# Causal attention in a 16-head, four-layer kernel: first-pass scores dealt to the steps of the second pass by a table

## The chip, the cores and the metric

The program runs on one core of a Trainium2 chip. A core has TensorE (PE in the profile), VectorE (DVE), ScalarE (ACT), GpSimd (POOL) and SyncE (SP), which here only issues DMAs. The metric is the device time of one execution in microseconds.

## The reference

Four layers are chained, each followed by a layer norm over 2 x 2048 tokens of 256 channels: causal attention with 16 heads of 16, an FP4-quantised linear layer, a second causal attention, and two blocks of local attention with a gated feed-forward. The change touches the two causal attentions, which share one function:

```python
q = (x @ Wq).reshape(b, t, h, d) * scale      # t = 2048, h = 16, d = 16
k = (x @ Wk).reshape(b, t, h, d) * scale
v = (x @ Wv).reshape(b, t, h, d)
dot = jnp.einsum('bqhd,bkhd->bhqk', q, k)
dot = jnp.where(causal[None, None], dot, -jnp.inf)
attn = jax.nn.softmax(dot, axis=-1)
out = jnp.einsum('bhqk,bkhd->bqhd', attn, v).reshape(b, t, h * d)
return out @ Wo
```

## The kernel before

The program loops twice over the batch and runs both causal attentions in each turn, so `attend` runs four times. Each time `project` has left q and k as three bf16 parts in `parts`, and six products of parts are stacked into 96 rows for the score matmuls (`stack_q`, `stack_k`). The 16 heads are four groups of four. A group's stacks are 48 DMAs (`load_stack`, L815); there are two sets of stacks, used in turn, and the first group's are loaded in `project`.

**Items and steps.** An item (`ITEMS`) is one group with one chunk of 512 queries: 16 items, with chunks 0, 1, 2, 3 in groups 0 and 2 and 3, 2, 1, 0 in groups 1 and 3. So the items have 4, 8, 12, 16, 16, 12, 8, 4, 4, 8, 12, 16, 16, 12, 8, 4 steps (`STEPS`, 160, numbered from 0). A step is one tile of 128 keys. The last four steps of an item lie on the diagonal, and there the width falls from 512 to 384, 256 and 128 queries. The text calls the last three of these the narrow steps of an item, and the other steps full.

**Second pass, the steps.** For each step PE makes scores with keys on the partitions, for four heads (L690, in two pairs of heads). ACT takes the exponential of each pair (L722) into one of two `probs` buffers. In the next step PE multiplies them with the values (L667, `pv`). For a diagonal block, POOL zeroes the masked half in between (L615). At an item's end ACT copies the outputs out of their bank (L714).

**First pass, the slots.** The exponential needs the row maximum to be taken off, and this rides as three extra rows of `stack_q`. So before an item's steps its maxima must be known. `first_pass_slots` lists the work: a slot fills one of three PSUM banks with scores that have queries on the partitions (L648, with a mask by L651), and DVE reads the bank once and keeps its maximum (L761 or L756). An item with chunk c has 11 + 16c such slots. After them comes a slot "maxima" (PE L638; DVE L776 to L785), in which DVE turns the maxima into three bf16 rows. After an item's end comes a slot "outputs" (PE L632, DVE L794 and L796). There are 560 score slots, 16 for maxima and 16 for outputs. PE may run three banks ahead of DVE (L627), and both take the slots in one order.

**What sets the place of a slot.** The list is fixed; the plan says how many slots go in front of step 0 and how many into each step. Before, the plan is computed (L92 to L107): each slot and step has a cost, each item's maxima are due `ROWS_LAG` = 4 steps before its first step, and slots are taken as late as these due times allow, at a rate of 1.1. That puts 68 slots in front. Inside a step PE runs (L678 to L700): scores of two heads, a quarter of the step's slots, scores of the other two, half of the slots, `pv` of the step before, the last quarter.

**SP.** After each item's maxima SP issues three DMAs of rows (L593), for which PE waits at the item's first step (L680). Behind the rows of some items SP loads the next group's stacks (L595 to L603): for group 1 all 48 DMAs stand behind the rows of item 0. PE waits for them before the first slot of the group's first item (L643).

Of the kernel before, what the change touches and what calls it, by code (L numbers as in the profile page):

```python
# [25 lines left out]
P = 128  # L26
NT = T // P
KT = C // P
CH = 512
NCH = T // CH  # L30
TPC = CH // P
# [5 lines left out]
GH = 4  # L37
# [29 lines left out]
ITEMS = [(g, c) for g in range(NG) for c in (range(NCH) if g % 2 == 0 else reversed(range(NCH)))]  # L67
STEPS = [(n, g, c, kt) for n, (g, c) in enumerate(ITEMS) for kt in range(TPC * (c + 1))]
# [2 lines left out]


TURN_LAG = 2
ROWS_LAG = 4
RATE = 1.1


def first_pass_slots():

    slots = []
    for n, (g, c) in enumerate(ITEMS):
        own = []
        for j in range(GH):
            own += [(n, (j, 1, i, cc)) for i in range(TPC) for cc in range(c)]

            own += [(n, (j, heads, i, c)) for i, heads in enumerate((4, 2, 1, 1)) if j % heads == 0]
        slots += own[:TURN_LAG] + ([(n - 1, "maxima")] if n else []) + own[TURN_LAG:]  # L90
    slots.append((len(ITEMS) - 1, "maxima"))
    fixed = 128  # L92
    cost = [fixed + (CH if what == "maxima" or what[3] < ITEMS[n][1] else what[1] * (what[2] + 1) * P)
            for n, what in slots]
    work = [GH * (fixed + CH - max(0, kt - TPC * c) * P) for n, g, c, kt in STEPS]
    slots_to, work_to = np.cumsum(cost), np.concatenate([[0], np.cumsum(work)])
    due = {}
    for n in range(len(ITEMS)):
        first = next(s for s, step in enumerate(STEPS) if step[0] == n)
        due[max(0, first - ROWS_LAG)] = slots.index((n, "maxima")) + 1  # L100
    plan, taken = [], 0
    for s in range(len(STEPS) + 1):
        need = max([slots_to[m - 1] - RATE * (work_to[d] - work_to[s]) for d, m in due.items() if d >= s] + [0])
        upto = len(slots) if s == len(STEPS) else max(taken, int(np.searchsorted(slots_to, need)) + (need > 0))
        turn = [(ITEM_END[s - 3], "outputs")] if s - 3 in ITEM_END else []
        plan.append(turn + slots[taken:upto])
        taken = upto  # L107
    plan.append([(len(ITEMS) - 1, "outputs")])
    return sum(plan, []), [0] + [int(n) for n in np.cumsum([len(p) for p in plan])]


SLOTS, SLOTS_TO = first_pass_slots()
MASKED = [m for m, (n, what) in enumerate(SLOTS) if len(what) == 4 and what[1] == 1 and what[3] == ITEMS[n][1]]
LAST_SLOT = {n: m for m, (n, what) in enumerate(SLOTS) if len(what) == 4}
# [448 lines left out]
def attend(k, parts, values, o, stacks, wo, wo_in):  # L563
# [10 lines left out]
    with ExitStack() as ctx:  # L574
# [11 lines left out]
        with nc.Block() as block:  # L586
            @block.sync
            def _(sp):
                sp.dma_start(wo[:, :, :], wo_in.rearrange("(t p) n -> p t n", p=P)).then_inc(S["w_in"], 16)
                for n, (g, c) in enumerate(ITEMS):  # L590
                    sp.wait_ge(S["max_split"], 4 * (n + 1))
                    for i in range(PARTS):
                        sp.dma_start(stacks[g % 2][0][KS + i:KS + i + 1, c, :, :], mrow[:, n % 2, i, :])\  # L593
                            .then_inc(S[f"rows{n}"], 16)
                    items = (0,) if g % 2 or not g else (1, 2)  # L595
                    if g + 1 < NG and n % NCH in items:
                        if g:
                            earlier = [s for s, step in enumerate(STEPS) if step[1] == g - 1]
                            sp.wait_ge(S["scores_kq"], 2 * (earlier[-1] + 1))
                        share = GH // len(items)  # L600
                        first = items.index(n % NCH) * share
                        for j in range(first, first + share):
                            load_stack(sp, parts, stacks[(g + 1) % 2], g + 1, j, S[f"stack{g + 1}"])  # L603
                sp.wait_ge(S["w_in"], 16)
# [206 lines left out]
def load_stack(eng, parts, stack, g, j, done):  # L811

    for s in range(NS):
        for dst, part, r0 in ((stack[0], Q_PART[s], 0), (stack[1], K_PART[s], 64)):
            eng.dma_start(dst[s * D:(s + 1) * D, :, j, :], parts[r0 + j * D:r0 + (j + 1) * D, g, part, :]).then_inc(done, 16)  # L815
# [942 lines left out]
```

## Time and profile before

| | us |
|---|---|
| median of 3 runs | 4344.6 |
| the three runs | 4340.57, 4344.6, 4346.11 |
| the profiled execution | 4337.45 |
| its span, first to last instruction | 4335.9 |
| the four attends, first score matmul to last exponential | 464.1, 464.3, 463.8, 464.3 |

The times of the four attends are read from the exponentials of L722: the first attend begins at 126.30 us, its step 0 at 174.51 us, and its last exponential ends at 590.37 us. A stretch of the trace from the first exponential of a step to that of another is called by the steps between.

### The profile page before, as it was taken

How to read it: one execution, taken by the hardware profiler on the slowest of the kernel's cores; microseconds unless marked ns; L12 is line 12 of the kernel's file. 1: busy time of each engine (PE TensorE's matmuls, PEld its weight loads, DVE VectorE, ACT ScalarE, POOL GpSimd, SP SyncE). 2: the span in 40 equal slices, each digit the busy share in tenths (PEclk: the TensorE clock that was granted, in tenths of full speed). 3: DMA queues.
4: the chain of work that ended last, by engine and by line, in shares of the span. 5: the costliest groups of instructions: out<-in, count | busy, mean ns of one | idle time of the engine just before them, and what ended most of it. 6: DMA issues, size and time to landing. Idle time of an engine off the chain costs nothing. (4 is left out here: it accounts for less than half of the span.)

```text
span 4335.9 us, 60351 instructions
## 1 busy us (share of the span) xinstructions
PE 3800.3 (88%) x19732; PEld 1809.3 (42%) x19732; DVE 2902.3 (67%) x7113; ACT 2045.6 (47%) x3685; POOL 895.6 (21%) x804
## 2 busy tenths in 40 slices
PE   7899978899978989898969999679999699888988
PEld 6233334233334545454543333343333355454545
DVE  3989766889756652666349896759896566436653
ACT  2366642366645541455124666324666455315541
POOL 1201013101023321332140010150010333213322
PEclk7799988799989999999988999788999899999999
DMA  3222002222010010000032220022220100100000
GB/s 78 44 31 31 1 2 49 33 30 31 1 62 6 1 49 7 22 6 1 25 69 30 31 31 1 2 51 30 31 31 1 62 6 1 50 26 6 1 10 25
DMA packets 129552, 108.89 MB, mean 25 GB/s; under 512 B 40872, under 2 KB 122320, under 8 KB 128208
## 3 DMA queue, kind: packets, MB, share of 16 engines
q1 hardware_dynamic: 129232, 104.92, 11.9%
q8 instruction: 164, 2.69, 0.3%
q14 instruction: 156, 1.28, 0.1%
HBM read 41.15 MB, written 4.19 MB: 10 GB/s over the span
## 5 line engine op out<-in xcount | busy, mean ns | idle before, releaser
L722 ACT ACTIVATE probs<-banks 128x1024 f32<-128x1024 f32 (+3 forms) x1280 | 1081.2, 895 | 755.2 <-PE banks L690 752.4
L761 DVE TENSOR_REDUCE chunk_max<-banks 128x1 f32<-128x512 f32 (+2 forms) x1728 | 1102.7, 684 | 72.3 <-PE banks L648 53.5
L648 PE MATMUL banks<-stack_k,stack_q 96*128 96x512 bf16 (+3 forms) x2560 | 824.9, 376 | 80.8 <-PEq L142 44.4
L690 PE MATMUL banks<-stack_q,stack_k 99*128 99x512 bf16 (+3 forms) x2560 | 661.6, 350 | 18.6 <-ACT probs L722 18.6
L667 PE MATMUL banks<-probs,values 128*17 128x512 f32 (+3 forms) x5120 | 591.8, 534 | 20.4 <-ACT probs L722 17.0
L648 PEld LDWEIGHTS banks<-stack_k,stack_q 96*128 96x128 bf16 x2560 | 241.2, 99 | 727.0 <-DVE chunk_max L761 402.2
L615 POOL TENSOR_SCALAR_AFFINE_SELECT probs<-probs 128x512 f32<-128x512 f32 x256 | 162.7, 635 | 1669.5 <-ACT probs L722 1666.3
L1320 ACT ACTIVATE probs_l<-probs_l,nmax 128x256 f32<-128x256 f32 x512 | 255.8, 500 | 454.6 <-DVE nmax L1437 454.6
L1217 PE MATMUL banks<-k_blocks,qT 128*128 128x512 f32 x512 | 291.5, 652 | 109.3 <-issue 103.8
L1197 PE MATMUL banks<-wqkv,hT 128*128 128x512 f32 x768 | 366.3, 616 | 2.7 <-issue 2.7
L690 PEld LDWEIGHTS banks<-stack_q,stack_k 99*128 99x128 bf16 x2560 | 232.4, 98 | 279.4 <-ACT probs L722 100.5
L1376 POOL TENSOR_TENSOR inv_norm<-ssum,mhalf 128x8 f32<-128x8 f32 x128 | 210.8, 1647 | 659.0 <-DVE ssum L1402 652.6
L1607 PE MATMUL banks<-hnT,w 128*128 128x512 f32 x704 | 313.6, 606 | 3.5 <-ACT hnT L1630 3.5
L756 DVE CUSTOM_DVE_ANT_0 masked_scores<-banks,wide_mask 128x384 f32<-128x384 f32 (+1 forms) x512 | 299.7, 617 | 17.5 <-PE banks L648 13.7
L1437 DVE CUSTOM_DVE_ANT_0 probs_l<-banks,later_keys 128x256 f32<-128x256 f32 x512 | 195.1, 418 | 118.6 <-PE banks L1217 118.6
L1636 ACT ACTIVATE gelu<-banks,b 128x512 f32<-128x512 f32 x80 | 55.0, 687 | 359.5 <-PE banks L1607 359.5
L1197 PEld LDWEIGHTS banks<-wqkv,hT 128*128 128x128 f32 x768 | 148.4, 200 | 168.9 <-issue 166.6
L1446 DVE RECIPROCAL rinv<-rsum 128x2 f32<-128x2 f32 x256 | 42.6, 166 | 260.5 <-ACT probs_l L1320 260.5
L1685 DVE SCALAR_TENSOR_TENSOR hidden<-banks,b,gelu 128x512 f32<-128x512 f32 x96 | 71.7, 749 | 205.6 <-ACT gelu L1636 197.6
L1607 PEld LDWEIGHTS banks<-hnT,w 128*128 128x128 f32 x704 | 136.9, 195 | 171.5 <-issue 165.8
L1618 PE MATMUL banks<-w,hidden 128*128 128x256 f32 x768 | 173.2, 386 | 14.9 <-DVE hidden L1685 14.9
L1378 POOL TENSOR_TENSOR prod_cos<-prod_cos,prod_sin 128x512 f32<-128x512 f32 x128 | 162.5, 1269 | 106.9 <-DVE prod_sin L1418 106.9
(188 smaller groups left out, 4865.7 us busy)
## 6 DMA issues: line engine op xcount, KB each, us to landing
stack_q<-parts SPq DMA_DIRECT2D x384, 64.0 KB, 2.4
stack_k<-parts SPq DMA_DIRECT2D x384, 64.0 KB, 2.4
xpos<-in_c_xpos SPq DMA_DIRECT2D x4, 2048.0 KB, 8.5
wqkv<-in_L_ffn_wqkv SPq DMA_DIRECT2D x12, 512.0 KB, 11.4
w<-in_L_ffn_w SPq DMA_DIRECT2D x16, 320.0 KB, 3.2
x_tok<-in_L_attn_x SPq DMA_DIRECT2D x8, 512.0 KB, 5.6
rope<-in_c_rope SPq DMA_DIRECT2D x2, 2048.0 KB, 7.6
hs_f<-x_mid SPq DMA_DIRECT2D x16, 256.0 KB
```

The lines of the kernel that those rows point to most:

```text
L648: ins = pe.matmul(out, sq[0:KS, c, j0 + j, i * P:(i + 1) * P], sk[0:KS, cc, j0 + j, 0:width], start=True, stop=not (diag and heads > 1), s ...
L667: ins = pe.matmul(ps[32 * j:32 * j + VW, PV, off:CH], values[:, kt, g * GH + j, :], probs[:, s % 2, j, off:CH], start=(kt == 0), stop=(s i ...
L690: ins = pe.matmul(ps[:, SCORE + j, off:CH], keys, sq[0:KS + PARTS, c, j, off:CH], start=True, stop=True, skip_group_check=True)
L722: act.activation(probs[:, s % 2, 2 * half:2 * half + 2, off:CH], ps[:, SCORE + 2 * half:SCORE + 2 * half + 2, off:CH], ACT.Exp)\
L756: dve.tensor_tensor_reduce(out=unread[:, at % 2, 0:width], in0=bank[:, 0:width], in1=wide_mask[:, CH - width:CH], scale=1.0, scalar=-3e38, ...
L761: dve.tensor_reduce(chunk_max[:, n % 2, j:j + heads, i, cc], bank[:, 0:heads * width].rearrange("p (h n) -> p h n", h=heads), AX.X, ALU.ma ...
L1197: ins = pe.matmul(ps[:, bank, :], hT[:, w % 2, t, 1 - t:P + 1 - t], wqkv[:, t, i * INNER:(i + 1) * INNER], start=(t == 0), stop=(t == KT - 1))
L1217: pe.matmul(ps[:, BS + n % 2, :].rearrange("p (a b n) -> p a b n", a=2, b=2), qT[:, p, :], kbd[:, p, :, s0:s1 + 1:s1 - s0, :], start=True, ...
L1320: ins = act.activation(pr[:, n % 2, h, :], pr[:, n % 2, h, :], ACT.Exp, bias=nmax[:, n % 2, h:h + 1], scale=-1.0, accum_out=rsum[:, n % 2, ...
L1376: pool.tensor_tensor(inv_n[:, own], ssum[:, own], mhalf[:, own], ALU.pow).then_inc(S["inv_n"], 1)
L1437: ins = dve.tensor_tensor_reduce(out=pr[:, n % 2, h, :], in0=ps[:, BS + n % 2, h * 2 * P:(h + 1) * 2 * P], in1=m, scale=1.0, scalar=3e38, ...
L1607: ins = pe.matmul(ps[:, bank + n % 2, :], w1[:, t, at:at + P], hT[:, t, :], start=(t == 0), stop=(t == KT - 1))
```

## The change

The computed plan is replaced by a table of 154 numbers, `FIRST_PASS_SHARE`. The first number is the count of slots in front of step 0, the next are the counts of steps 0 to 152. They add up to 576, all slots but those for outputs, which stay where they were. The order of the slots is the same; only the steps to which they go differ. In front stand 24 slots (item 0, its maxima, 12 of item 1) where there were 68. The stacks of group 1 are loaded in two halves, behind the rows of items 1 and 2.

```diff
-ROWS_LAG = 4
-RATE = 1.1
+FIRST_PASS_SHARE = (
+    24,
+    5, 8, 4, 9, 5, 5, 9, 11, 5, 3, 2, 3, 6, 5, 5, 5, 6, 7, 7, 6,
...
+)
@@ first_pass_slots
     plan, taken = [], 0
     for s in range(len(STEPS) + 1):
-        need = max([slots_to[m - 1] - RATE * (work_to[d] - work_to[s]) for d, m in due.items() if d >= s] + [0])
-        upto = len(slots) if s == len(STEPS) else max(taken, int(np.searchsorted(slots_to, need)) + (need > 0))
+        upto = taken + FIRST_PASS_SHARE[s] if s < len(FIRST_PASS_SHARE) else len(slots)
@@ attend, SP
-                    items = (0,) if g % 2 or not g else (1, 2)
+                    items = (0,) if g % 2 else (1, 2)
```

How many slots (maxima included, outputs not) each stretch holds:

| stretch | before | after |
|---|---|---|
| in front of step 0 | 68 | 24 |
| steps 0 to 3 (item 0) | 12 | 26 |
| steps 4 to 11 (item 1) | 31 | 43 |
| steps 12 to 23 (item 2) | 42 | 60 |
| steps 24 to 55 (items 3, 4) | 110 | 125 |
| steps 56 to 79 (items 5 to 7) | 93 | 80 |
| steps 80 to 119 (items 8 to 11) | 138 | 141 |
| steps 120 to 159 (items 12 to 15) | 82 | 77 |

PE at the end of the front and in steps 0 and 1, before. L648 and L651 are slots, L690 the scores of a step, L667 its product with the values.

```order
79 L648 MATMUL banks<-stack_k,stack_q 128x384
80 L648 MATMUL banks<-stack_k,stack_q 128x512 x7
81 L690 MATMUL banks<-stack_q,stack_k 128x512 x2
82 L648 MATMUL banks<-stack_k,stack_q 128x512
83 L690 MATMUL banks<-stack_q,stack_k 128x512 x2
```

The same place in the changed kernel, where the lines are one lower (L647 slots, L689 scores).

```order
51 L647 MATMUL banks<-stack_k,stack_q 128x384
52 L647 MATMUL banks<-stack_k,stack_q 128x512 x5
53 L689 MATMUL banks<-stack_q,stack_k 128x512 x2
54 L647 MATMUL banks<-stack_k,stack_q 128x384
55 L689 MATMUL banks<-stack_q,stack_k 128x512 x2
56 L647 MATMUL banks<-stack_k,stack_q 128x512 x4
```

Step 0 now comes 28 rows earlier, and it has more slots around it.

PE in steps 36 to 40 before, the end of item 3 (L638 is the maxima's transpose).

```order
317 L638 MATMUL banks<-identf,neg_max 16x128
318 L690 MATMUL banks<-stack_q,stack_k 128x512 x4
319 L667 MATMUL banks<-probs,values 17x512 x4
320 L690 MATMUL banks<-stack_q,stack_k 128x384 x4
321 L667 MATMUL banks<-probs,values 17x512 x4
322 L690 MATMUL banks<-stack_q,stack_k 128x256 x4
323 L667 MATMUL banks<-probs,values 17x384 x4
324 L690 MATMUL banks<-stack_q,stack_k 128x128 x4
325 L667 MATMUL banks<-probs,values 17x256 x4
326 L690 MATMUL banks<-stack_q,stack_k 128x512 x4
```

The changed kernel in steps 36 to 38.

```order
311 L689 MATMUL banks<-stack_q,stack_k 128x512 x2
312 L647 MATMUL banks<-stack_k,stack_q 128x512
313 L637 MATMUL banks<-identf,neg_max 16x128
314 L666 MATMUL banks<-probs,values 17x512 x4
315 L647 MATMUL banks<-stack_k,stack_q 128x512 x2
316 L689 MATMUL banks<-stack_q,stack_k 128x384 x4
317 L666 MATMUL banks<-probs,values 17x512 x4
318 L647 MATMUL banks<-stack_k,stack_q 128x512
319 L689 MATMUL banks<-stack_q,stack_k 128x256 x2
320 L647 MATMUL banks<-stack_k,stack_q 128x512
321 L689 MATMUL banks<-stack_q,stack_k 128x256 x2
```

Steps 36 to 41 had no score slot; now they hold 5, 1, 4, 2, 4 and 4.

## Rows read from the trace of the kernel before

**Rows 1.** Page, part 1: busy time, share, instructions of each engine.

```profile
PE 3800.3 (88%) x19732; PEld 1809.3 (42%) x19732; DVE 2902.3 (67%) x7113; ACT 2045.6 (47%) x3685; POOL 895.6 (21%) x804
```

**Rows 2.** Busy time by stretch: front and steps, first and last attend.

```profile
core 0: us, PE busy (x) PEld busy (x) DVE busy (x) ACT busy (x) POOL busy (x), PEclk, DMA share, GB/s
126.30:174.50 48.20, 39.91 (x107) 11.38 (x108) 47.75 (x101) 0.00 (x0) 6.73 (x1) 0.50 0.42 66
174.50:590.40 415.90, 401.14 (x2642) 135.17 (x2640) 334.53 (x717) 276.06 (x335) 40.04 (x63) 1.00 0.11 17
...
2914.50:2962.70 48.20, 39.87 (x107) 11.43 (x108) 47.73 (x101) 1.28 (x1) 6.76 (x1) 0.50 0.42 67
2962.70:3378.80 416.10, 401.35 (x2643) 135.31 (x2640) 334.55 (x717) 276.05 (x335) 40.03 (x63) 0.99 0.11 17
```

**Rows 3.** Busy time by item, first attend: items 0 to 2, 14, 15.

```profile
174.51:183.99 9.48, 9.48 (x56) 3.67 (x55) 7.75 (x15) 5.41 (x9) 2.55 (x4) 0.80 0.20 31
183.99:205.48 21.49, 20.97 (x142) 7.34 (x141) 20.44 (x43) 13.49 (x17) 2.54 (x4) 1.00 0.01 2
205.48:237.09 31.61, 30.89 (x194) 9.82 (x193) 27.63 (x56) 21.11 (x25) 2.54 (x4) 1.00 0.01 2
...
565.16:583.83 18.67, 16.41 (x114) 4.97 (x113) 7.35 (x25) 13.24 (x18) 2.54 (x4) 1.00 0.01 2
583.83:590.37 6.54, 5.05 (x42) 1.66 (x40) 0.68 (x2) 5.57 (x9) 1.90 (x3) 1.00 0.00 0
```

**Rows 4.** Busy time: steps 24-35, 37-39, 9-11, 40-41, 56-64.

```profile
237.09:272.59 35.50, 35.34 (x215) 11.69 (x214) 33.50 (x65) 23.85 (x25) 0.00 (x0) 1.00 0.01 1
274.44:279.93 5.49, 4.54 (x37) 1.41 (x38) 0.00 (x0) 3.25 (x8) 2.54 (x4) 1.00 0.07 10
199.70:205.48 5.78, 5.78 (x45) 1.94 (x44) 5.60 (x10) 3.25 (x6) 1.90 (x3) 1.00 0.00 0
...
279.93:284.57 4.64, 3.99 (x29) 1.27 (x28) 0.40 (x2) 4.26 (x6) 0.00 (x0) 1.00 0.69 102
...
322.97:350.95 27.98, 27.49 (x186) 10.18 (x185) 26.38 (x77) 17.94 (x19) 0.70 (x1) 1.00 0.01 2
```

**Rows 5.** DVE in order of time, in the front.

```profile
start us, us, engine line op out<-in xcount [idle before <-releaser]
127.15 5.97 DVE L734 CAST wide_mask<-mask_qk 128x128 f32<-128x128 bf16 x1
...
140.71 0.27 DVE L776 COPY max_rows_f<-banks 16x128 f32<-16x128 f32 x1
...
142.03 2.46 DVE L761 TENSOR_REDUCE chunk_max<-banks 128x1 f32<-128x512 f32 x4
```

**Rows 6.** PE in order of time, steps 41 and 42.

```profile
282.46 1.05 PE L667 MATMUL banks<-probs,values 128*17 128x512 f32 x8
283.44 0.66 PE L632 MATMUL banks<-identf,o_dims 128*128 128x128 f32 x4
283.93 0.60 PE L690 MATMUL banks<-stack_q,stack_k 99*128 99x512 bf16 x2
284.37 0.38 PE L648 MATMUL banks<-stack_k,stack_q 96*128 96x512 bf16 x1
284.59 0.59 PE L690 MATMUL banks<-stack_q,stack_k 99*128 99x512 bf16 x2
```

**Rows 7.** Waits in the first attend.

```profile
ACT probs L722 <- PE banks L690: 190.1, 144, 51.0
```

**Rows 8.** SP in order of time, the front; then the rows' DMAs to landing.

```profile
142.13 1.83 SPq L593 DMA_DIRECT2D stack_q<-max_rows  x3
144.01 0.65 SPq L815 DMA_DIRECT2D stack_q<-parts  x1
...
175.21 0.60 SPq L815 DMA_DIRECT2D stack_k<-parts  x1
175.85 1.86 SPq L593 DMA_DIRECT2D stack_q<-max_rows  x3
...
DMA to landing us min/median/max: 1.6/1.7/3.8
```

**Rows 9.** Busy time and granted clock as the steps begin.

```profile
174.50:177.00 2.50, 2.50 (x10) 1.19 (x9) 1.72 (x4) 2.05 (x2) 0.05 (x1) 0.50 0.69 104
177.00:179.00 2.00, 2.00 (x8) 0.73 (x6) 1.78 (x6) 1.13 (x2) 0.59 (x1) 0.67 0.06 12
```

More of the change, by code:

```diff
@@ L91, in first_pass_slots @@
     slots.append((len(ITEMS) - 1, "maxima"))
[L92 to L100, printed above, removed]
     plan, taken = [], 0
     for s in range(len(STEPS) + 1):
-        need = max([slots_to[m - 1] - RATE * (work_to[d] - work_to[s]) for d, m in due.items() if d >= s] + [0])
-        upto = len(slots) if s == len(STEPS) else max(taken, int(np.searchsorted(slots_to, need)) + (need > 0))
+        upto = taken + FIRST_PASS_SHARE[s] if s < len(FIRST_PASS_SHARE) else len(slots)
         turn = [(ITEM_END[s - 3], "outputs")] if s - 3 in ITEM_END else []
```

7 rows, old and new, of the table FIRST_PASS_SHARE are left out of this document.

## The prediction

> **What bounds the kernel now.** First the page's busy times: PE 88%, DVE 67%, ACT 47% [rows 1]. That is a mean over unlike stages, so the next view is the busy time by stretch. It shows four attends that are alike to 0.5 us, each a front of 48.2 us and 160 steps of 416 us [rows 2]; together they are 1857 of 4336 us. Nothing outside them is touched.
>
> In the front DVE is busy 47.75 of 48.20 us, ACT does nothing, and PE runs at a granted clock of 0.50, which is 1.2 GHz [rows 2]. So DVE sets the front. In order of time it first spends some 7 us on the mask and then reads bank after bank. Four reads of 512 columns take 2.46 us together, about 0.60 us from one to the next once the overlap of 0.08 is counted; a maxima slot takes from 140.71 to 142.03, 1.32 us [rows 5].
>
> In the steps PE is busy 401 of 416 us, DVE 335, ACT 276 [rows 2]. PE's busy time overstates, since its matmuls overlap; the distance between starts is the price. The product with the values takes 0.98 us (282.46 to 283.44), the four transposes of an outputs slot 0.49, a pair of score matmuls 0.44, a slot 0.22 [rows 6]. So a full step costs PE about 0.98 + 0.88 = 1.86 us and each slot 0.22 more, while a slot costs DVE 0.60. The two are even at 1.86 / (0.60 - 0.22), about 5 slots a step: below that PE leads, above it DVE. ACT needs about 2.0 us per full step (23.85 us in twelve of them [rows 4]), and its waits for PE's scores, 190 us, are the other side of this: 51.0 of them are the front and the wait before it [rows 7].
>
> By item, DVE is busy 20.44 of 21.49 us in item 1 (95%) and 27.63 of 31.61 in item 2, and in items 14 and 15 nearly nothing [rows 3]. **The work is ill spread**: DVE alone in front, PE and ACT with idle DVE near the end.
>
> **Part A: the front and steps 0 to 23.** 44 slots leave the front and go into steps 0 to 23. By the counts of the change, 153 slots lie ahead of step 24 in both kernels (68+12+31+42 and 24+26+43+60), and the outputs slots of items 0 and 1 too. So DVE's work up to step 24 is the same: 47.75 + 7.75 + 20.44 + 27.63 = 103.6 us [rows 2, 3]. Before, it took 48.2 + 9.48 + 21.49 + 31.61 = 110.8 us. The front itself shrinks by 43 x 0.60 + 1.32 = 27 us, but that is not the gain: in items 0 to 2 the change has 129 slots in 24 steps, 5.4 a step, and 9, 9 and 11 in steps 3, 6 and 7. By the balance above DVE is then last there, and what the front gives the steps take back. The gain is only DVE's idle time, 7.2 us at most. DVE is busy 99% in the front and 95% in item 1, the two stretches of before where it leads. At 99% the stretch takes 104.6 us, at 95% 109.0. I take 97.5%, 106.2 us, between them, since both kinds of stretch are in it: **a gain of 4.6 us**, bounds 1.8 and 6.2.
>
> In that value are two small losses. Step 0 starts at 1.2 GHz, as before; the clock rose about 4 us later, after PE had been busy without a break [rows 9], and step 0 with its slots takes PE twice its time until then. And the rows of item 1, which before were long there, are now made in step 3, one step ahead of their use: three issues of 1.83 us together and a landing of 1.7 us [rows 8] against the 8 slots behind them, 8 x 0.60 = 4.8 us of DVE's work; PE runs up to three banks ahead of this, so it may wait about 0.5 us. What stands behind that wait in PE's queue is step 4 and its slots, and DVE has up to three banks left to read. The rows of item 0 cost nothing: issued at 142.13, landed by about 145.7, while PE has ten more slots ahead of step 0 (to about 146).
>
> SP: the 48 loads of group 1 ran from 144.01 to 175.8, and item 1's rows behind them at 175.85 [rows 8]. In the old place they would now hold up item 1 by over 20 us; in halves of 24 x 0.64 = 15.4 us behind the rows of items 1 (step 3) and 2 (step 9) they end before the next rows are made: steps 4 to 8 carry 35 slots, 21 us. The second half lands some 20 us after step 9, and group 1's first slot is in step 20, 50 slots or 30 us later. Cost nothing; the cover is 9 us.
>
> **Part B: steps 24 to 159.** They took 590.37 - 237.09 = 353.3 us and hold 423 slots in both kernels. Prices from pieces of the trace [rows 4]: the three narrow steps of an item take 5.49 us with no slot and 5.78 with 8, so a slot costs 0.04 us there. They are bound by the chain of scores, exponential, mask and product, not by PE. Two full steps without score slots take 4.64, 2.32 each; the twelve steps 24 to 35, with 54 slots counting one for outputs, 35.50, 2.96 each with 4.5 slots. The stretch of two has one outputs slot, 0.5 a step, so the first four slots of a step cost 0.64 / 4 = 0.16 each, and further ones 0.22. Steps 56 to 64, with 42 slots, three maxima among them, take 27.98 / 9 = 3.11 us each, with DVE busy 94%: there DVE leads and a slot costs up to 0.60.
>
> Items 3 and 4 gain 15 slots: 13 into the empty full steps 36, 40 and 41 (+2.1), 7 into narrow steps (+0.3), 5 fewer elsewhere (-1.1): +1.3 us, and more likely +1.7 since the counts are uneven. Items 5 to 7 lose 13, part of them at DVE's price: at a mean of 0.36, -4.7. Items 8 to 11 are moved little: -0.5. Items 12 to 15 lose 5 (-1.1), put 10 into narrow steps (10 x 0.18 = -1.8) and 14 into empty full steps (14 x 0.06 = -0.8): -3.7. Sum, with 1.7 for the first: **-7.2 us**.
>
> A second way gives more. PE's pure work of items 3 to 15, by the distances above, is 314 us; filled steps run 0.1 us over it each (35.50 us in steps 24 to 35, against 12 x 1.86 + 53 x 0.22 + 0.49 = 34.5). If the full steps of the change ran as near to PE, 13 us in all, and the narrow steps and the last items kept some 12 us of their idle time, items 3 to 15 would take 339 us, a gain of 14. I take 9, near the first, because it rests on measured pieces of the same kind. Bounds 0 (the unevenness of the table eats it) and 14.
>
> **Sum.** (4.6 + 9) x 4 = 54 us. The profiled execution took 4337.45, so it would take 4283; the median of the runs lies 7 us above that execution, so I forecast **4290** for the median, a gain of 1.25%.
>
> **Rivals.**
> 1. *Both engines stay fed.* DVE at 99% in part A (6.2) and PE at 0.1 us a step over its work in part B (14): 20.2 x 4 = 81, 4264. For it: with three banks between them PE rarely starves DVE where it leads. Against: full steps before are filled evenly and only reach 95%.
> 2. *Only part A comes.* Steps with 2 or 3 slots beside ones with 5 or 6 may cost as much as the empties they replace: 4.6 x 4 = 18, 4326. For it: PE needs only 1.86 us and 0.22 a slot in a step of few slots but ACT 2.0 at least, so short steps save less than long ones add.
> 3. *The clock falls in steps 1 to 11; slower than before.* [...] If items 0 and 1 ran at 1.2 GHz, PE would need twice 32 us, 64, where DVE needs 43: 20.5 us more, less the 13.6 gained, +7 x 4 = 28 us, 4372. It decides from two thirds of these items on. Against it: at 1.2 GHz PE is busy without a break there, and that is what preceded the rise before [rows 9]. A partial fall, 4 us an attend, leaves 4306. The Trainium skill (TensorE: Matmul & The Clock Gate, section "A second HAM failure mode: psum-queue depth-cycling") says that a TensorE which cycles through PSUM banks with many micro-idles swings between its two clocks; by that rule the three-bank queue ahead of DVE is where it would happen. No such swing is in the steps of before, whose clock is 1.00 throughout after the first.
> 4. *The change doesn't do what it says.* DVE could starve because item 1's or group 1's data come late; the covers of 0.5 us short and 9 us long leave no room for more than a few us.
>
> **Chances.** Forecast 0.52, rival 1 0.25, rival 2 0.13, rival 3 in full 0.06, anything else 0.04 (half of it no change). The range 4250 to 4328 takes in the forecast and rivals 1 and 2 and leaves out the rest with some error of the terms. A measurement of this kernel can tell about 0.2%, 9 us, from no change. Faster 0.90, same 0.03, slower 0.07.
>
> **What the profile after would show.** Front: about 21.5 us, DVE busy all of it. Items 0 to 2: about 85 us in place of 62.6, DVE busy over 95%, clock 1.00 from 4 us after step 0 on. Steps 24 to 159: about 344 in place of 353, with steps 37 to 39 still near 5.6 us and steps 56 to 64 near 25 in place of 28. The forecast is wrong if DVE idles over 5% in items 0 to 2, if the clock column shows 0.50 there, or if the irregular steps of items 9 to 13 are no shorter than before.

## The result and the profile after

| | before | after |
|---|---|---|
| median, us | 4343.1 (4 runs) | 4289.8 (4 runs, 4286.3 to 4296.0) |
| the profiled execution | 4337.45 | 4286.33 |
| ratio | | 0.9879, 95% interval 0.9865 to 0.9894 |

The change makes the kernel 1.2% faster, 53 us, and the forecast was 4290. (One run of before was added beside the runs of after, so its median is now 4343.1.)

Busy time by stretch of the changed kernel, first attend: the front, item 0, item 1, item 2; then the second attend's item 0. Columns as in [rows 2].

```profile
125.48:146.96 21.48, 14.86 (x50) 5.50 (x51) 21.18 (x42) 0.00 (x1) 6.76 (x1) 0.50 0.05 13
146.96:164.74 17.78, 15.29 (x81) 5.58 (x80) 16.41 (x37) 5.52 (x8) 2.55 (x4) 0.81 0.04 7
164.74:193.56 28.82, 26.91 (x147) 8.12 (x146) 27.58 (x60) 13.58 (x18) 2.57 (x4) 0.94 0.36 54
193.56:231.60 38.04, 36.51 (x222) 12.20 (x221) 37.84 (x76) 21.29 (x26) 2.54 (x4) 1.00 0.27 42
...
781.24:801.01 19.77, 17.49 (x80) 6.37 (x79) 17.40 (x38) 5.53 (x9) 2.54 (x4) 0.67 0.10 15
```

The front fell from 48.2 us [rows 2] to 21.5, and items 0 to 2 grew from 62.6 [rows 3] to 84.6. Together 110.8 became 106.1, with DVE busy 103.0 of it, where it was 103.6. The clock column has changed: item 0 has 0.81, as before (0.80), but over 17.8 us in place of 9.5, and item 1 has 0.94 where it had 1.00 [rows 3]. In the second and fourth attend item 0 took 19.8 us at a mean of 0.67.

The pieces of steps 24 to 159, first attend: steps 37-39, 56-64, and items 12, 13 and 14.

```profile
269.72:275.69 5.97, 5.97 (x54) 2.46 (x53) 5.80 (x11) 3.26 (x6) 1.91 (x3) 1.00 0.05 8
319.73:344.95 25.22, 24.70 (x171) 9.18 (x170) 21.42 (x64) 17.94 (x19) 0.21 (x2) 1.00 0.01 3
484.13:523.62 39.49, 39.49 (x265) 13.23 (x264) 30.01 (x61) 28.94 (x34) 2.82 (x5) 1.00 0.01 1
...
523.62:551.57 27.95, 27.44 (x187) 8.78 (x186) 17.58 (x43) 21.19 (x26) 2.39 (x4) 1.00 0.01 2
551.57:568.25 16.68, 15.71 (x111) 4.69 (x110) 6.10 (x19) 13.43 (x18) 2.70 (x5) 1.00 0.01 2
```

Steps 56 to 64 fell from 27.98 to 25.22, with DVE busy 85% where it was 94% [rows 4]. Item 14 fell from 18.67 [rows 3] to 16.68. All of steps 24 to 159 took 343.2 us in place of 353.3.

The totals per attend, in us, over the four attends of each trace:

| stretch | before | after | gain |
|---|---|---|---|
| front + items 0 to 2 | 110.8, 111.1, 110.5, 111.1 | 106.1, 107.2, 105.8, 107.3 | 4.3 mean |
| items 3, 4 (means from here on) | 85.9 | 88.1 | -2.2 |
| items 5 to 7 | 65.4 | 61.0 | 4.4 |
| items 8 to 11 | 105.0 | 103.4 | 1.6 |
| items 12 to 15 | 97.0 | 90.9 | 6.1 |
| the four attends | 1856.5 | 1799.9 | 56.6 in all |
| all the rest of the program | 2479.5 | 2484.8 | -5.3 in all |

The difference in the last row is not the change's: in the traces of the twelve experiments below, which all leave the rest of the program as it is, the same remainder lies between 2474.5 and 2486.2. I did not find what moves it. So the attends are the better measure of an edit, and the tables below give them.

### The profile page after: what moved, and what is told of

It reads as the page before. It is cut to its first block and busy times, and to the rows that moved or that the text cites. A ratio compares the mean times of both kernels' runs of the same rounds, so it can differ in the third digit from the quotient of the medians.

```text
span 4284.7 us, 60351 instructions
## 1 busy us (share of the span) xinstructions
PE 3755.8 (88%) x19732; PEld 1804.7 (42%) x19732; DVE 2914.2 (68%) x7113; ACT 2050.1 (48%) x3685; POOL 896.4 (21%) x804
## 5 line engine op out<-in xcount | busy, mean ns | idle before, releaser
L647 PE MATMUL banks<-stack_k,stack_q 96*128 96x512 bf16 (+3 forms) x2560 | 794.9, 365 | 93.3 <-PEq L141 44.4
L689 PE MATMUL banks<-stack_q,stack_k 99*128 99x512 bf16 (+3 forms) x2560 | 644.5, 351 | 4.8 <-ACT probs L721 3.0
L647 PEld LDWEIGHTS banks<-stack_k,stack_q 96*128 96x128 bf16 x2560 | 239.2, 99 | 750.0 <-DVE chunk_max L760 427.7
L1216 PE MATMUL banks<-k_blocks,qT 128*128 128x512 f32 x512 | 292.9, 655 | 109.4 <-issue 104.0
L689 PEld LDWEIGHTS banks<-stack_q,stack_k 99*128 99x128 bf16 x2560 | 237.8, 99 | 231.4 <-ACT probs L721 39.8
```

Source lines behind the costliest of these rows:

```text
L647: ins = pe.matmul(out, sq[0:KS, c, j0 + j, i * P:(i + 1) * P], sk[0:KS, cc, j0 + j, 0:width], start=True, stop=not (diag and heads > 1), s ...
L689: ins = pe.matmul(ps[:, SCORE + j, off:CH], keys, sq[0:KS + PARTS, c, j, off:CH], start=True, stop=True, skip_group_check=True)
L1216: pe.matmul(ps[:, BS + n % 2, :].rearrange("p (a b n) -> p a b n", a=2, b=2), qT[:, p, :], kbd[:, p, :, s0:s1 + 1:s1 - s0, :], start=True, ...
```

## The experiments

**Theory.** DVE reads each bank once, wherever the slot stands. Up to step 24 DVE is last in any order, so what counts there is only its idle time. After it PE leads, and the gain comes from slots moved out of a stretch where DVE leads (items 5 to 7) and into steps that had room (ends of items, items 12 to 15). **Rival:** the shorter front is the gain, and the later steps only give part of it back.

### One part at a time

The first experiment keeps the table up to step 23 and takes the computed plan's numbers from step 24 on. The second does the reverse, with the loads in their old place. Both hold 153 slots before step 24, so they join without a change.

```diff
 # a_front, against after: from step 24 on
-    5, 2, 3, 3, 3, 5, 4, 4, 5, 4, 5, 4, 6, 3, 5, 2, 5, 1, 4, 2,
+    5, 2, 3, 3, 4, 5, 4, 5, 4, 5, 4, 5, 4, 4, 5, 4, 0, 0, 0, 0,
...
 # b_rest, against after: up to step 23
-    24,
-    5, 8, 4, 9, 5, 5, 9, 11, 5, 3, 2, 3, 6, 5, 5, 5, 6, 7, 7, 6,
+    68,
+    4, 4, 3, 1, 5, 4, 5, 4, 5, 3, 3, 2, 4, 5, 4, 5, 4, 4, 5, 4,
-                    items = (0,) if g % 2 else (1, 2)
+                    items = (0,) if g % 2 or not g else (1, 2)
```

> The table's numbers for the front and steps 0 to 23, the computed plan's from step 24 on, the new place of the loads. Part A alone. My sum: 4.7 us an attend as in the trace after (110.8 to 106.1), so 4343 - 19 = 4324. If the front's shortening of 27 us an attend were the gain and the later steps only took it back by their unevenness, more would be left here, up to 4250. If part A and part B only work together, 4343.

> The computed plan's numbers for the front and steps 0 to 23 with the loads in their old place, the table's from step 24 on. Part B alone. My theory: 10 us an attend, items 3 to 15 as in the trace after (343.2 us in place of 353.3), so 4303. If the two parts are not additive, clearly away from 4343 - 40.

a_front: 4326.7 against 4338.2, ratio 0.9973 (0.9963 to 0.9982). b_rest: 4297.9 against 4338.2, ratio 0.9910 (0.9894 to 0.9927). In the attends a_front saves 11.3 us, all before step 24, and b_rest 39.2, nearly all after it. The stretch that an experiment leaves alone kept its time: 353.2 to 353.3 us for a_front's steps 24 to 159, 110.5 to 110.6 for b_rest's front and items 0 to 2. a_front is below the forecast (11.3, not 19), because its stretch took 107.2, 107.3, 110.0 and 107.6 us. The attend with 110.0 has 10.2 us at the lower clock in items 0 and 1, of which more below. In it and in the first one PE also waits for item 1's rows, 0.8 and 1.4 us. The line of the first attend, items 0 and 1:

```profile
PE banks L689 <- DMA stack_q<-max_rows: 1.4, 1, 1.4
```

The busy time of a_front's steps 24 to 159, and of b_rest's front, first attend:

```profile
234.03:587.33 353.30, 339.80 (x2253) 114.41 (x2251) 278.47 (x605) 236.07 (x285) 32.42 (x51) 1.00 0.13 19
```

```profile
125.48:173.73 48.25, 39.91 (x107) 11.44 (x108) 47.78 (x101) 0.00 (x1) 6.76 (x1) 0.50 0.42 66
```

So the parts nearly add (50.5 of after's 56.6 us), and the larger is B: the visible part of the change, the front cut by 27 us, carries about a quarter of the gain, by this pair. The rival falls: it had up to 4250 for a_front.

### The front's length

```diff
 # front40, against after
-    24,
-    5, 8, 4, 9, 5, 5, 9, 11, 5, 3, 2, 3, 6, 5, 5, 5, 6, 7, 7, 6,
+    40,
+    5, 4, 4, 5, 5, 5, 5, 7, 5, 3, 2, 3, 6, 5, 5, 5, 6, 7, 7, 6,
```

> The changed kernel with 16 of the slots moved back to the front: 40 in front, 4 fewer in each of steps 1, 3, 6 and 7. DVE theory: DVE sets the whole stretch to step 24, so front + items 0 to 2 stay at 106 us an attend within 1, though the front is 9.6 us longer; 4290, or up to 2 us an attend less where the clock no longer falls in items 0 and 1 (4282). Rival, the front's length is what counts: + 9.6 x 4 = 4328.

4276.2 against 4338.2, ratio 0.9865 (0.9849 to 0.9882). The front is 9.3 us longer, and front and items 0 to 2 together take 106.6, 105.5, 105.3 and 104.5, mean 105.5, where after has 106.6. The rival, 4328, is out: **the length of the front by itself is worth nothing**. Front and items 0 to 2 of its fourth attend:

```profile
2871.74:2902.56 30.82, 23.95 (x69) 7.44 (x70) 30.49 (x65) 1.28 (x1) 6.76 (x1) 0.50 0.03 9
2902.56:2914.70 12.14, 11.18 (x69) 4.18 (x68) 11.31 (x24) 5.54 (x8) 2.56 (x4) 0.88 0.27 41
2914.70:2937.93 23.23, 22.26 (x139) 7.42 (x138) 22.96 (x50) 13.43 (x18) 2.61 (x4) 1.00 0.35 52
2937.93:2976.26 38.33, 36.63 (x222) 12.20 (x221) 38.12 (x76) 21.29 (x25) 2.55 (x4) 1.00 0.27 41
```

DVE is busy 102.9 of 104.5 us. Item 1's clock is at 1.00 again in all four attends. The total also came out 13.6 us lower than after's median, but the runs of before beside it were 5 us lower too, and the two ratios are not told apart. In the traces the attends are 3 us shorter than after's and the remainder of the program 7 us.

### Group 1's loads in their old place

```diff
 # loads_old, against after
-                    items = (0,) if g % 2 else (1, 2)
+                    items = (0,) if g % 2 or not g else (1, 2)
```

> The changed kernel with group 1's 48 loads behind the rows of item 0 as before. Theory: item 1's rows wait for 48 x 0.64 = 31 us of issues from about step 0 on, where the first item's steps take 18, so PE stands some 10 to 15 us at item 1's first step: +40 to +60 us, about 4340. If the covers are longer than I think, 4290.

4344.5 against 4341.2, ratio 1.0005 (0.9995 to 1.0016): the whole gain is gone. The longest waits of PE in its items 0 and 1 (from 147 to 200 us), and item 0:

```profile
PEld banks L689 <- DMA stack_q<-max_rows: 13.7, 1, 13.7
PE banks L689 <- DMA stack_q<-max_rows: 13.3, 1, 13.3
```

```profile
147.48:179.36 31.88, 16.06 (x80) 5.73 (x79) 17.15 (x38) 5.53 (x9) 2.55 (x4) 0.66 0.61 92
```

PE stands 13.3 us for item 1's rows (11.8 to 13.3 over the attends); item 0 takes 31.7 to 32.2 us in all four attends, and front and items 0 to 2 take 121.3 us in place of 106.6. So the second edit, one line of SP's loop, is what lets the first one work.

### Where part B's gain is

b_mid has the table's numbers in steps 24 to 79 only, b_late from step 117 on only. Both have the old front and loads.

```diff
 # b_mid, against before's numbers from step 24; step 80 has 2 in place of 4
-    4, 5, 4, 5, 4, 5, 4, 5, 4, 4, 5, 4, 0, 0, 0, 0,
+    3, 5, 4, 4, 5, 4, 5, 4, 6, 3, 5, 2, 5, 1, 4, 2,
...
 # b_late, against before's numbers from step 116
-    0, 0, 0, 0, 0, 0, 4, 4, 5, 4, 5, 4, 5, 4, 5, 4, 0, 0, 0, 0,
+    0, 1, 4, 0, 4, 2, 2, 3, 3, 3, 3, 6, 2, 2, 1, 5, 2, 3, 3, 1,
...
```

> The old plan with the table's numbers in steps 24 to 79 (items 3 to 7) only, two slots fewer in step 80, loads in their old place. Forecast from the trace after: items 3 and 4 +2.2, items 5 to 7 -4.4, so -2.2 us an attend, 4334. If VectorE does not lead in items 5 to 7 and the gain comes from elsewhere, 4343 or slower.

> The old plan with the table's numbers from step 117 on (items 12 to 15 and the narrow steps of item 11), loads in their old place. Forecast: items 12 to 15 -6.3 us an attend as in the trace after, and +0.7 since 4 more slots must be held, so 4320. Rival: the empty steps cost nothing to leave empty, 4343.

b_mid: 4325.6 against 4341.2, ratio 0.9967 (0.9954 to 0.9980). b_late: 4317.1, ratio 0.9947 (0.9929 to 0.9964). Items 3 and 4, then 5 to 7 of b_mid, and items 12 to 15 of b_late, first attend:

```profile
236.98:325.12 88.14, 87.09 (x568) 29.90 (x567) 81.25 (x168) 57.90 (x66) 4.93 (x8) 1.00 0.25 37
325.12:386.11 60.99, 59.22 (x420) 21.85 (x419) 53.35 (x131) 40.32 (x51) 7.77 (x13) 1.00 0.01 2
```

```profile
494.16:585.81 91.65, 87.74 (x602) 28.38 (x600) 54.36 (x124) 69.13 (x84) 9.81 (x16) 1.00 0.01 2
```

b_mid's two stretches are those of after to the tenth: 15 slots into items 3 and 4 cost 2.2 us, 13 out of items 5 to 7 give 4.4. Of b_mid's 15.5 us only 8.6 are in the attends, as forecast. The remainder of the program is 5 us shorter in its trace, and 2 us are the difference between medians and profiled executions. b_late's 91.65 us are 1.0 more than after's 90.67: in its first and third attend PE waits 0.9 us for the rows of item 15, and in the second and fourth, without that wait, the stretch takes 90.6 as in after. b_late saves 20.1 in the attends, 5 an attend, about half of b_rest's 39.2.

### Do the uneven numbers matter?

```diff
 # smooth, against after (first of seven rows; same sums per item and in narrow steps)
-    5, 2, 3, 3, 3, 5, 4, 4, 5, 4, 5, 4, 6, 3, 5, 2, 5, 1, 4, 2,
+    5, 2, 3, 3, 5, 4, 3, 5, 4, 4, 5, 4, 4, 5, 4, 4, 4, 1, 4, 2,
...
```

> The changed kernel with the slots of items 3 to 14 dealt evenly over the full steps of each item, same counts per item and in the narrow steps. Theory: the price of a slot does not depend on its neighbours, so 4290 within 4 us. Rival: the table's uneven numbers fit the places where the steps have room, and even ones lose up to 2 us an attend (4298). Other rival: unevenness costs, and even ones win as much (4282).

4286.2 against 4341.2, ratio 0.9877 (0.9860 to 0.9895), after's own ratio to 0.0002. Steps 24 to 159 of its first attend:

```profile
232.44:575.74 343.30, 336.42 (x2253) 114.58 (x2251) 282.47 (x606) 236.80 (x285) 32.66 (x51) 1.00 0.13 20
```

343.3 us, where after had 343.2. In sum it doesn't matter where in the full steps the slots of an item are. By pieces it does a little: smooth is 0.9 us shorter in items 3 and 4 and 0.4 in items 8 to 11, and 0.4 and 0.9 longer in items 5 to 7 and 12 to 15 (means of four attends), so each of the two rivals holds somewhere, and they cancel.

### The mask at the head of the front

The front begins with three operations of DVE before the first bank is read; the last is a cast of 128x128 that takes 5.97 us [rows 5]. In the same microseconds GpSimd fills the ones rows of the second stacks. The edit makes the fill wait for the mask.

```diff
 # mask_first, against after; before_mask, against before
+                pool.wait_ge(S["mask_in"], 2)
                 pool.memset(stacks[1][1][KS:KS + PARTS, :, :, :], 1.0).then_inc(S["ones_rows"], 1)
```

> The changed kernel, with GpSimd's fill of the ones rows (6.92 us) held back until VectorE has made the mask. The cast of the mask (128x128, L734) takes 5.97 us at the head of each front, while GpSimd's fill runs. If the cast is held up by that fill, it takes some 0.3 us here and each attend's front is 5.6 us shorter: 4290 - 22 = 4268. If the cast is slow by itself, 4290. Later reads of banks may be held up by the fill in turn: then the front is as long as before.

> The kernel before, with only GpSimd's fill held back behind the mask. Front 42.6 us in place of 48.2, all else as before: 4341 - 22 = 4319. If the fill then slows VectorE's reads of the banks, less, down to 4341.

mask_first: 4269.4 against 4338.2, ratio 0.9843 (0.9826 to 0.9859). before_mask: 4312.7 against 4340.1, ratio 0.9936 (0.9919 to 0.9952), its attends 23.9 us shorter in all. DVE in order of time in after, then in mask_first:

```profile
126.36 5.97 DVE L733 CAST wide_mask<-mask_qk 128x128 f32<-128x128 bf16 x1
132.36 1.29 DVE L760 TENSOR_REDUCE chunk_max<-banks 128x4 f32<-128x512 f32 x2
```

```profile
127.68 0.17 DVE L734 CAST wide_mask<-mask_qk 128x128 f32<-128x128 bf16 x1
127.96 1.29 DVE L761 TENSOR_REDUCE chunk_max<-banks 128x4 f32<-128x512 f32 x2
```

The fill in after, then in mask_first:

```profile
125.32 6.92 POOL L607 MEMSET stack_k<- 3x8192 bf16 x1 [1.33 <-POOLq L141]
```

```profile
127.91 6.92 POOL L608 MEMSET stack_k<- 3x8192 bf16 x1 [2.60 <-DVE wide_mask L734]
```

In after the cast starts 1.04 us behind the fill and ends at 132.33, 0.09 us behind the fill's end. It takes 0.17 us when the fill does not run. The fill is as long as before and runs beside DVE's reads of the banks without slowing them: front 15.76 us in place of 21.48. This agrees with the Trainium skill (SBUF — State Buffer, section "Who interferes with whom"): a cast may enter a mode of VectorE that takes a pair of ports shared with GpSimd, the engine that comes second is blocked for the whole instruction of the first, and reductions never contend. The edit shortens the front by 5.7 us in both plans.

In the kernel before all of this reaches the attends (23.9 us in four). In mask_first only 13.4 us of 22.9 do: items 0 to 2 grew. Item 1 of its first and of its third attend:

```profile
161.54:191.96 30.42, 28.59 (x147) 8.86 (x146) 27.19 (x58) 13.91 (x18) 2.60 (x4) 0.88 0.32 49
```

```profile
2270.81:2298.16 27.35, 25.35 (x147) 7.74 (x146) 26.89 (x58) 13.69 (x17) 2.60 (x4) 1.00 0.35 53
```

The same work, 3.1 us apart: DVE's busy time is 27.19 against 26.89, and what differs is the granted clock, 0.88 against 1.00. In all four attends PE also waits for item 1's rows, as item 0 ends: 0.3 to 0.5 us, and in the third 1.4.

### The clock in items 0 and 1

```diff
 # mask_even, against mask_first
-    5, 8, 4, 9, 5, 5, 9, 11, 5, 3, 2, 3, 6, 5, 5, 5, 6, 7, 7, 6,
+    7, 7, 6, 6, 6, 6, 6, 6, 5, 5, 5, 4, 6, 5, 5, 5, 6, 7, 7, 6,
 # mask_front40, against mask_first: the two rows of front40
 # mask_front48, against mask_first
-    24,
-    5, 8, 4, 9, 5, 5, 9, 11, 5, 3, 2, 3, 6, 5, 5, 5, 6, 7, 7, 6,
+    48,
+    4, 4, 3, 3, 4, 5, 5, 5, 4, 3, 2, 3, 6, 5, 5, 5, 6, 7, 7, 6,
```

> mask_first with the 26 slots of item 0 dealt 7, 7, 6, 6 and the 43 of item 1 dealt 6, 6, 6, 6, 5, 5, 5, 4, in place of 5, 8, 4, 9 and 5, 5, 9, 11, 5, 3, 2, 3; the front still 24. If bursts of 9 and 11 slots starve TensorE and bring its clock down, the stretches at 0.50 in item 1 vanish and front + items 0 to 2 take 100 to 101 us in all four attends (now 100.4 once and 103.8 three times): 4260. If it is the share of VectorE's work over the whole of items 0 and 1, they stay and the time is 4270.

> The changed kernel with both edits: GpSimd's fill held back behind the mask, and 40 slots in front with 4 fewer in steps 1, 3, 6 and 7. If the two gains add (5.6 us an attend for the mask, 1 to 2 for the clock), front + items 0 to 2 take 100 us an attend and the kernel 4255. If the earlier start of the front only brings back the low clock in items 0 and 1, 4265.

> mask_front40 with 48 slots in front and 4, 4, 3, 3, 4, 5, 5, 5, 4 in steps 0 to 8. VectorE's work to step 24 is the same, so if it is last there in any case, front + items 0 to 2 stay at 98 to 101 us an attend and the kernel at 4254; with the clock up 3 to 4 us after step 0 in all four attends, 4250. If TensorE now leads in items 0 and 1, VectorE idles there and the time turns up, 4260.

| | us | ratio (95%) | front + items 0 to 2, four attends | item 1 |
|---|---|---|---|---|
| mask_first | 4269.4 | 0.9843 (0.9826, 0.9859) | 103.8, 104.0, 100.4, 103.7 | 30.4, 30.3, 27.4, 30.4 |
| mask_even | 4264.5 | 0.9828 (0.9812, 0.9845) | 100.0, 101.0, 99.3, 104.2 | 27.5, 27.3, 27.5, 27.6 |
| mask_front40 | 4254.1 | 0.9811 (0.9792, 0.9829) | 98.9, 101.4, 99.5, 98.3 | 23.2 four times |
| mask_front48 | 4260.7 | 0.9820 (0.9803, 0.9836) | 101.0, 100.3, 99.0, 101.5 | 21.0 four times |

In mask_first the clock falls to 0.50 in three attends, 16 us after step 0, in step 3, and comes back 10.2 us later, in step 5. With the slots of items 0 and 1 dealt evenly, item 1 takes 27.3 to 27.6 us in all four attends, and what is left of these falls is 3.4 us in step 3, in two attends. So the uneven dealing of the slots brought the long falls, by four attends of each. Of the bursts it can only have been those of steps 1 to 3 (8, 4 and 9 slots), since the 9 and 11 of steps 6 and 7 come after the clock is back. mask_even also makes item 1's rows one step earlier, in step 2, and PE's wait for them is gone; in mask_first the fall comes before that wait (158.8 against 160.15 us), so the wait is not its cause. What decides whether the clock falls is not shown. The 10.2 us before the fall in mask_first's first attend, and the same steps of its third attend, where no fall followed:

```profile
148.60:158.80 10.20, 7.71 (x52) 2.43 (x51) 10.03 (x25) 1.97 (x5) 1.90 (x3) 1.00 0.02 4
2258.00:2268.20 10.20, 7.71 (x55) 2.61 (x53) 9.99 (x24) 1.85 (x4) 1.70 (x3) 1.00 0.02 4
```

PE is busy 7.71 us in both, and DVE nearly without a break: TensorE stands between banks while DVE works the slots off. Item 2 of mask_even's fourth attend lost 2.6 us (40.6 in place of 38.0), which is why its sum is 104.2; that trace has two more stretches of 3.4 us at the lower clock, as item 2 begins and as it ends, and I have no cause for their place. With 40 slots in front both gains add. With 48 nothing more comes, by the trace of its first attend, item 0:

```profile
155.70:165.64 9.94, 9.94 (x65) 4.32 (x64) 8.37 (x18) 5.31 (x9) 2.56 (x4) 0.82 0.62 93
```

DVE idles 1.6 of 9.9 us, PE is never idle: PE leads again, so DVE is not last in every order. **mask_front40 beats both kernels**, 1.9% under before. mask_even, mask_front40 and mask_front48 are so close that the intervals do not settle their order.

## Why the prediction was right

- **Part A**, "DVE's work up to step 24 is the same" and only its idle time can be had: right. Forecast 4.6 us an attend, measured 4.3; forecast 106.2 for the stretch, measured 105.8 to 107.3. front40 shows the mechanism directly.
- **The start at 1.2 GHz, "as before"**: wrong in size. The clock rose 3.8 us after step 0 before; now it rises after 6.6 us in the first attend (6.3 to 7.2 in the four), and item 0 has 0.67 in two attends. The profile has PE busy without a break over those 6.6 us as well, so what preceded the rise in [rows 9] did not bring it as early here; the cause is open. The 97.5% taken for DVE covered the loss by luck: 97.1% was measured in the first attend (103.0 of 106.1).
- **Rival 3, the clock falls in steps 1 to 11**: it came in the partial form, so one of the prediction's signs of being wrong, 0.50 in the clock column of items 0 to 2, did appear. In the first and third attend it is 3.4 us in step 7, which has 11 slots; in the second and fourth 6.8 us that begin in step 3, which has 9. The full form did not come. The price was less than the 4 us an attend of the partial rival: front40, where the clock does not fall again once it is up, took 1.1 us less than after, and in mask_first a fall of 10.2 us, 7.5 of them in item 1, cost 3.1 us there.
- **The rows of item 1**, about 0.5 us: no idle time of PE for these rows shows in after, but a_front has 1.4 and 0.8 us in two attends and mask_first 0.3 to 1.4 in all four, so after was lucky here. What the prediction left out is **the rows of item 15**, whose maxima moved from step 151 to 152: PE waits 0.7 us for them in after's third attend, and 0.6 to 1.1 in the first and third attend of most experiments with the table's last steps. **The loads**: the forecast of "over 20 us" in the old place was too high, 13.3 us measured. The prediction's own terms give 16: item 1's rows would land 53 us after the front's start, and the front with the 26 slots of item 0 takes 37. That the new place costs nothing held.
- **Part B, items 3 and 4**: forecast +1.7, measured +2.2. **Items 5 to 7**: -4.7, measured -4.4; DVE's lead there was the right reason, as its busy share fell from 94% to 85%. **Items 8 to 11**: -0.5, measured -1.6; 1.4 of it is item 9, which holds 3 slots fewer and takes 20.08 us in place of 21.49. Before, DVE was busy 20.44 us of those 21.49, so these slots had nearly DVE's price, 0.47 each, and the prediction gave none of it to this item.
- **Items 12 to 15** were mis-sized: -3.7 in the prediction, -6.1 measured. The term that failed is the price of a slot in a full step, "the first four slots of a step cost 0.16 each". It was drawn from two empty steps (2.32 us each) to steps with 4.5 slots (2.96) as if the line between were straight. In after the steps between exist. Steps 124 to 126, with 3 slots each, steps 128 and 129, with 2 each, and step 130, with 1, first attend:

```profile
494.45:502.21 7.76, 7.76 (x46) 2.20 (x45) 5.84 (x12) 5.82 (x7) 0.00 (x0) 1.00 0.00 0
505.62:510.40 4.78, 4.78 (x29) 1.27 (x28) 3.04 (x6) 3.88 (x5) 0.00 (x0) 1.00 0.00 0
510.40:512.57 2.17, 2.17 (x14) 0.54 (x13) 0.69 (x2) 1.94 (x3) 0.00 (x0) 1.00 0.00 0
```

That is 2.59 us a step with 3 slots, 2.39 with 2 and 2.17 with 1; the straight line from 2.24 (2.32 less the 0.08 of half an outputs slot) gives 2.72, 2.56 and 2.40. So inside an item a slot costs PE's 0.22, and the foot of the line was wrong: the two empty steps it was drawn from, 40 and 41, are the first two of an item. Inside an item a step without score slots (138) takes 1.95 us, not 2.32. Why the first steps of an item are longer is not shown. The ten inner steps 122 to 131 of item 12, 44 slots before and 30 after:

```profile
498.05:527.39 29.34, 29.34 (x178) 9.59 (x177) 27.24 (x54) 19.39 (x21) 0.00 (x0) 1.00 0.00 1
```

```profile
489.46:515.55 26.09, 26.09 (x154) 7.49 (x153) 19.14 (x36) 19.38 (x20) 0.00 (x0) 1.00 0.00 1
```

Over items 12 to 14, first attend, 39 slots left such inner steps for 9.3 us, 0.24 each. 18 went into the first two steps of an item for 2.0 us, 0.11 each, and 16 into the last four for 1.0 us, 0.06 each: in sum -6.3. The prediction had 29 slots leaving at 0.22; it counted 14 into empty full steps, where 24 went to the first two or the last full one, and that is some 0.6 us of what it missed. The end of an item is cheap as a whole. Steps 116 to 119, the last full step of item 11 and its narrow ones, in before and in after:

```profile
486.07:493.40 7.33, 6.35 (x49) 1.66 (x48) 1.09 (x5) 5.10 (x8) 2.54 (x4) 1.00 0.01 2
```

```profile
476.31:484.13 7.82, 7.82 (x58) 2.55 (x57) 6.50 (x17) 5.19 (x8) 2.38 (x4) 1.00 0.01 2
```

Nine slots more for 0.49 us, where the prediction's prices give 4 x 0.16 + 5 x 0.04 = 0.84. The "second way", PE's work with its usual excess, gave 14 for the whole of part B; the measured 10.1 lies between the two ways.
- **Rivals 1 and 2** (4264, 4326): neither. smooth shows that the reason given for rival 2, that uneven steps cost, does not hold in sum.
- The sum was aided by chance at one place: the attends gained 56.6 us, not 54, and the rest of the program happened to be 5 us longer in that trace.

## What to carry to other kernels

When one engine is last over a whole stretch, moving its work about inside the stretch is worth only its idle time there; count its busy time across both orders before counting the microseconds by which a visible stage shrinks. Price a moved instruction by the place it leaves and the place it goes to: here a slot cost 0.60 us where DVE alone led (the front), 0.22 where PE led, and 0.05 at an item's end, where a chain of waits led. Take the base of such a price from the same kind of place: the empty steps at the head of an item misled here. And look at any short operation that takes long beside one of another engine: a 128x128 cast of 5.97 us was worth 23.9 us in the four attends of the kernel before, for one line of code.

## What was not expected of the hardware

A VectorE cast of 128x128 from bf16 to fp32 in SBUF took 5.97 us while a GpSimd fill of 3 partitions ran, and 0.17 us without it; VectorE's reductions of PSUM banks ran beside the same fill at full speed. TensorE's clock stayed at 0.50 or fell back to it in stretches in which the profile calls TensorE 87% busy (step 7 of after, 8.15 us with a mean clock of 0.79):

```profile
176.48:184.63 8.15, 7.13 (x27) 1.97 (x27) 7.21 (x15) 2.05 (x3) 0.00 (x0) 0.79 0.23 35
```

27 matmul instructions in 8.15 us are few, and the busy time overstates: a slot's matmul counts 0.38 us where the next starts after 0.22 [rows 6]. In mask_first's front the clock stayed at 0.50 with PE busy 14.76 of 15.76 us. The Trainium skill (TensorE: Matmul & The Clock Gate, section "A second HAM failure mode: psum-queue depth-cycling") describes such swings for a TensorE that cycles through PSUM banks. The traces here fit: the falls in items 0 and 1 come where it waits on the three-bank queue, and they shrink when the slots are dealt evenly. One is of another kind: in loads_old the clock is at 0.50 for 20.5 to 23.9 us around the wait of 12 to 13 us for item 1's rows. A few falls of 3.4 to 6.8 us appear late in the steps of some traces as well. All six stand in item 15 of a first or third attend, just after PE waited 0.7 to 1.1 us for that item's rows; eleven other attends have such a wait and no fall, so the wait is not shown to be the cause.
